# One head-group step of an attention kernel in another order: one call with the values, transposes and score products rearranged, waits left out

## The reference

```
q = rope(layernorm(x) @ Wq)            # 32 heads of 8 columns
k, v = split(ctx @ Wkv);  k = rope(k)
w = softmax(q @ k.T / sqrt(8))         # per batch and head, 256 x 256
x = x + tanh(g_xattn) * ((w @ v) @ Wout + bout)
x = x + tanh(g_ffn) * experts(layernorm(x))   # 2 shared, 32 routed, 6 of them per token
```

## Time and profile before

| what | value |
|---|---|
| median of 3 runs | 475.64 us |
| profiled execution, its own time | 475.44 us |
| its span | 473.6 us |
| TensorE busy, of the span | 448.4 us (95%) |
| VectorE busy | 286.7 us (61%) |
| ScalarE busy | 199.0 us (42%) |
| first score product starts | 40.35 us |
| last normalisation ends | 187.45 us |

### The profile page before, as it was taken

The page is one execution under the profiler, slowest core; times in us unless marked ns, Lnnn a source line. Parts: engine busy times, 40 slices in busy tenths (PEclk is TensorE's granted clock), DMA queues, the critical chain, the costliest instruction groups (busy, mean ns, idle before and its releaser), DMA issues.

```text
span 473.6 us, 8151 instructions
## 1 busy us (share of the span) xinstructions
PE 448.4 (95%) x2515; PEld 335.4 (71%) x2515; DVE 286.7 (61%) x574; ACT 199.0 (42%) x366; POOL 144.1 (30%) x233
## 2 busy tenths in 40 slices
PE   5788999999999998888899999999999999999996
PEld 5356666666666665566688888888888888888885
DVE  7897977877777674640445555455554455554455
ACT  1467777787877565471222222222222222222221
POOL 9046800000000000245144333444333444334430
PEclk9799999999999999999899999999999999999999
DMA  8012111111111100999852323333223322334102
GB/s 220 15 47 48 35 32 34 35 32 32 30 32 35 24 1 11 329 333 316 205 150 89 89 89 100 116 93 89 89 89 111 110 89 89 89 93 125 48 0 90
DMA packets 34056, 43.62 MB, mean 92 GB/s; under 512 B 5633, under 2 KB 28209, under 8 KB 34033
## 3 DMA queue, kind: packets, MB, share of 16 engines
q1 hardware_dynamic: 30737, 42.07, 31.1%
q10 hardware_dynamic: 3296, 1.25, 1.1%
HBM read 37.93 MB, written 1.18 MB: 83 GB/s over the span
## 4 chain that ended last, share of the span: by engine, by line
PE 85%; DVE 7%; ACT 3%; DMA 2%; issue 1%; POOL 1%; DVEq 0%; SPq 0%; POOLq 0%; ACTq 0%
PE psum L1126 26%; PE psum L1111 26%; PE psum L962 8%; PE psum L975 7%; PE psum L938 6%; PE psum L925 3%; PE psum L949 2%; PE psum L881 2%; PE psum L1024 2%; PE psum L890 1%; DVE nmax L716 1%; DVE ang L619 1%; PE psum L853 1%; PE psum L986 1%; DMA G<-gates_by_expert 1%
## 5 line engine op out<-in xcount | busy, mean ns | idle before, releaser
L591 ACT ACTIVATE hh<-hu 128x512 fp32r<-128x512 f32 x88 | 55.6, 633 | 186.7 <-DVE hu L822 186.7
L822 DVE SCALAR_TENSOR_TENSOR hu<-psum,b1cols,G 128x512 f32<-128x512 f32 x88 | 65.9, 751 | 110.3 <-PE psum L1111 101.3
L716 DVE TENSOR_REDUCE nmax<-psum 128x2 f32<-128x512 f32 x128 | 85.2, 687 | 25.9 <-PE psum L938 24.6
L492 ACT ACTIVATE probs<-psum 128x512 f32<-128x512 f32 x128 | 69.4, 595 | 14.1 <-PE psum L962 13.7
L1126 PE MATMUL psum<-hh,w2h 128*128 128x512 f32 (+1 forms) x188 | 73.3, 390 | 1.3 <-DVE hl L828 1.3
L1126 PE MATMUL psum<-hl,w2h 128*128 128x512 f32 (+1 forms) x188 | 73.2, 389 | 0.0
L1126 PE MATMUL psum<-hh,w2l 128*128 128x512 f32 (+1 forms) x188 | 73.1, 389 | 0.0
L828 DVE SCALAR_TENSOR_TENSOR hl<-hu,hh 128x512 fp32r<-128x512 f32 x88 | 60.3, 687 | 9.6 <-ACT hh L591 9.6
L1111 PE MATMUL psum<-xTh,w1h 128*128 128x512 f32 (+1 forms) x188 | 58.8, 394 | 2.2 <-POOL w1l L405 1.5
L1111 PE MATMUL psum<-xTh,w1l 128*128 128x512 f32 (+1 forms) x188 | 58.8, 394 | 0.0
L1111 PE MATMUL psum<-xTl,w1h 128*128 128x512 f32 (+1 forms) x188 | 58.5, 392 | 0.0
(11 more groups left out here) (148 smaller groups left out, 550.3 us busy)
## 6 DMA issues: line engine op xcount, KB each, us to landing
G<-gates_by_expert SPq DMA_DIRECT2D x40, 256.0 KB, 3.9
w<-in_L_ffn_rw_dram SPq DMA_DIRECT2D x4, 1408.0 KB, 13.4
w<-in_L_ffn_rw_dram SPq DMA_DIRECT2D x2, 2816.0 KB, 17.5
G<-gates_by_expert SPq DMA_DIRECT2D x8, 448.0 KB, 3.5
Kd<-QK SPq DMA_DIRECT2D x104, 32.0 KB, 1.9
G<-gates_by_expert SPq DMA_DIRECT2D x8, 384.0 KB, 3.5
G<-gates_by_expert SPq DMA_DIRECT2D x8, 320.0 KB, 3.4
G<-gates_by_expert SPq DMA_DIRECT2D x8, 192.0 KB, 3.7
```

The costliest lines, as they stand in the source:

```text
L492: act.activation(probs[g % 2][:, kt, 2 * hp:2 * hp + 2, :], ST_BANK[(4 * g + n) % 3][:, :].rearrange("p (h q) -> p h q", h=2), ACT.Exp, sc ...
L591: act.activation(hh[(SHT + j) % 2][:, cols], hu[2 * j + half][:, :], ACT.Relu).then_inc(rhh_ok, 1)
L716: dve.tensor_reduce(nmax[i % 2][:, qt, 2 * hp:2 * hp + 2], S_BANK[n % 2][:, :].rearrange("p (h k) -> p h k", h=2), AX.X, ALU.max, negate=T ...
L822: dve.scalar_tensor_tensor(out=hu[2 * (j % 2) + half][:, :], in0=H_BANK[2 * (j % 2) + half], scalar=b1cols[:, bass.ds(it * len(G) + j, 1)] ...
```

## The change

Six things change, all in the attention loop.

1. `values(i)` is one call: the eight matmuls of both halves follow one another, and each half still waits for its exponentials.
2. TensorE's order in a step is new. A step begins with `scores(i, 2)`. T2 stands between this product and `scores(i, 3)`. The first two products of the next group stand between shifted scores. The transposes for the group 3 ahead stand in front of the last shifted score.
3. ScalarE copies `oT` before a step's four exponentials, which follow one another.
4. VectorE takes all four row maxima and `maxima` before it normalises. `variances` of batches 0 to 2 moves behind the loop.
5. Transposed attention, projection and residual of batches 0 to 2 move to steps 11, 19, 27 and 12, 20, 28. The tile `attnT` lies in two other places of `Vx` for this.
6. Waits that others imply are left out. The wait for the copied keys moves from the first score product to the second transpose of T2, a step earlier than the keys are read, and at the start to the third product.

Before the change the first such residual stands behind step 28's maxima. The diff, cut to its core:

```diff
@@ constants
-        ATTN_STEPS = [GROUPS - 5, GROUPS - 3, GROUPS - 1]
-        PROJ_STEPS = [GROUPS - 4, GROUPS - 2, GROUPS - 1]
-        RESIDUAL_STEPS = [GROUPS - 4, GROUPS - 2, GROUPS - 1]
+        ATTN_STEPS = [NG * (b + 1) + 3 for b in range(B - 1)]
+        PROJ_STEPS = [n + 1 for n in ATTN_STEPS]
+        RESIDUAL_STEPS = PROJ_STEPS
@@ ScalarE, step(i)
                     evacuate_t(i + AHEAD)
-                if 0 <= g < GROUPS:
-                    exponentials(g, 0)
-                    exponentials(g, 1)
                 p = (i - 3) // 2
                 if i % 2 and 0 <= p < PAIRS:
-                    act.wait_ge(pv_mm, 2 * (i - 1))
-                    if p >= 2:
-                        act.wait_ge(ot_mm, p - 1)
+                    act.wait_ge(pv_mm, i - 1)
                     act.activation(oT[p % 2][:, :], O_BANK[:, 0:N], ACT.Copy).then_inc(o_ok, 1)
-                if i in ATTN_STEPS[1:]:
+                if i in ATTN_STEPS:
                     transposed_attention(ATTN_STEPS.index(i))
                 if 0 <= g < GROUPS:
-                    exponentials(g, 2)
-                    exponentials(g, 3)
-                if i == ATTN_STEPS[0]:
-                    transposed_attention(0)
+                    for n in range(4):
+                        exponentials(g, n)
@@ VectorE
                     row_max(i, 2)
+                    row_max(i, 3)
+                    maxima(i)
                 if i >= 4 and i % 2 == 0:
                     normalise((i - 4) // 2)
-                if i < GROUPS:
-                    row_max(i, 3)
-                    maxima(i)
                 if i in RESIDUAL_STEPS:
                     residual(RESIDUAL_STEPS.index(i))
-                if i == RESIDUAL_STEPS[-1]:
-                    variances(0, NT - TB)
+
+            variances(0, NT - TB)
@@ TensorE, transposed_with_max(i)
-                if i >= 1:
-                    pe.wait_ge(q2_ok, i)
...
                 for t in range(TB):
+                    if t and i + 2 < GROUPS:
+                        keys_copied(i + 2)
                     ins = pe.transpose(T2_BANK[:, t * P:(t + 1) * P],
@@ TensorE, values
-            def values(i, kt):
+            def values(i):
...
+                for kt in range(TB):
+                    pe.wait_ge(exp_ok, 4 * i + 2 * (kt + 1))
+                    for h in range(GH):
@@ TensorE, the loop
                 if i == 0:
+                    keys_copied(0)
                     scores(i, 0)
                     scores(i, 1)
-                if weighted:
-                    values(i - 2, 0)
+                    transposes(AHEAD)
+                    keys_copied(1)
+                if new:
+                    scores(i, 2)
                 if shifted:
                     transposed_with_max(i - 1)
...
                 if new:
-                    scores(i, 2)
+                    scores(i, 3)
+                if weighted:
+                    values(i - 2)
+                if i in ATTN_STEPS:
+                    attention_transposed(ATTN_STEPS.index(i))
+                if i in PROJ_STEPS:
+                    output_projection(PROJ_STEPS.index(i))
                 if i >= 4 and i % 2 == 0:
                     outputs((i - 4) // 2)
+                if i + 1 < GROUPS:
+                    scores(i + 1, 0)
                 if shifted:
                     shifted_scores(i - 1, 0)
                     shifted_scores(i - 1, 1)
...
+                if i + 1 < GROUPS:
+                    scores(i + 1, 1)
                 if shifted:
                     shifted_scores(i - 1, 2)
+                if i + 1 + AHEAD < GROUPS:
+                    transposes(i + 1 + AHEAD)
+                if shifted:
                     shifted_scores(i - 1, 3)
```

More of the change, by code:

```diff
@@ L964, in shifted_scores @@
                 ins.then_inc(st_mm, 1)
-            def values(i, kt):
+            def values(i):
                 b, g = i // NG, i % NG
-                pe.wait_ge(exp_ok, 4 * i + 2 * (kt + 1))
                 second = i % 2
-                if kt == 0 and not second and i:
-                    pe.wait_ge(o_ok, i // 2)
-                for h in range(GH):
-                    ins = pe.matmul(O_BANK[HR * h:HR * h + HR, 0:N], Vx[:, TB * b + kt, GH * g + h, :], probs[i % 2][:, kt, h, :],
-                                    start=(kt == 0 and not second), stop=(kt == TB - 1 and bool(second)),
-                                    skip_group_check=True)
+                for kt in range(TB):
+                    pe.wait_ge(exp_ok, 4 * i + 2 * (kt + 1))
+                    for h in range(GH):
+                        ins = pe.matmul(O_BANK[HR * h:HR * h + HR, 0:N], Vx[:, TB * b + kt, GH * g + h, :], probs[i % 2][:, kt, h, :],
+                                        start=(kt == 0 and not second), stop=(kt == TB - 1 and bool(second)),
+                                        skip_group_check=True)
                 ins.then_inc(pv_mm, 1)
             def outputs(p):
-                pe.wait_ge(o_ok, p + 1)
-                pe.wait_ge(q2_ok, min(2 * p + 4, GROUPS))
-                if p:
+                if 2 * p + 4 <= GROUPS:
+                    pe.wait_ge(q2_ok, 2 * p + 4)
+                else:
+                    pe.wait_ge(o_ok, p + 1)
                     pe.wait_ge(norm_ok, p)
```

49 lines of the change are left out of this document (13 added, 36 removed).

## The result

The changed kernel takes 468.98 us (median of 4, 467.25 to 470.71), before takes 475.35 (median of 4, 474.84 to 475.83): ratio 0.9866 [0.9827, 0.9906], 6.4 us less. Two later series of the changed kernel, 469.59 and 469.33, lie just inside it, so on which side of 469.0 the kernel falls is a matter of the runs' spread; the term that was off is not. The profiled execution took 467.25 us, its span is 465.2.

What follows compares the result with a forecast made beforehand. TensorE bounds the attention loop (busy 103.86 of 104.00 us) and stays the bound, narrowly. Terms -9.75 + 1.2 + 4.45 + 0.6 = -3.5 us take 475.44 to 471.9, or 472.1 against the median; range 469.0 to 476.8.

Steps and rivals of the forecast that it cites:

- The step: Attention loop: mean step 3.85 us against 4.176, saving 0.325 in each of 30 steps, -9.75 us.
- rival B: Inside merged `values`: a weight load of 0.11 stands open in each of 30 calls, 3.3 us back, 475.4; chance 0.12.
- Its parts: Within a step: one merged `values` call saves 0.27 us, and `QT` no longer in a hurry saves about 0.07.
- The margin of 0.1 for VectorE: Two row maxima end 0.35 into the next step, and `scores(i,3)` wants that bank at 0.45.
- Attention and projection: Steps 11 to 13 and their like, three batches: 6.95 us of stalls against 2.5 before, +4.45 us.
- the sign that the prediction had named for being wrong in the stalls: Step 12, with the projection: less than 1.9 us lost there would show the stalls wrong.
- rival C: Exponentials end the step: at 0.65 each, 0.2 to 0.25 us a step is lost, 478.6, slower; chance 0.13.
- the two waits for `QK`: TensorE waits for `QK`, copied near 2.1 us into a step: 0.35 lost in step 11, 0.4 in step 12.
- The start: Third product waits 0.5 us for group 1's keys; T2 of group 1 is 0.9 to 1.4 late: +1.2 us.
- The end: Group 31's exponentials queue behind group 30's; T2 to last normalisation goes from 6.8 to 7.4 us: +0.6.
- The waits left out: Attention loop: they cost nothing before, since each was met when its matmul came: 0.
- Rival E: Projection steps stall no more than before, since VectorE catches up: 4 us more gained, 468.1; chance 0.09.

Runs made afterwards that it cites:

- e1: Kernel before with only the merge of both `values` halves, all else in the old order: 474.29 us, ratio 0.9978.
- e2: Changed kernel with `values` in two halves again, the next group's first score product between them, except in attention and projection steps: 478.96 us, ratio 1.01.
- e8: Changed kernel with scores(i+1, 1) moved behind the last shifted score, so two score products stand side by side again: 483.89 us, ratio 1.0163.
- e4: Changed kernel with `outputs` ahead of the projection: 468.45 us, ratio 0.983.
- e6: Changed kernel with `outputs` ahead of the projection and the statistics of batches 0 to 2 in step 32: 465.97 us, ratio 0.9769.
- e7: Changed kernel with all the waits that the change left out put back: 470.29 us, ratio 0.9885.
- a0_again: The changed kernel timed again, nothing edited: 469.59 us, ratio 0.9873.
- e3_late_proj: Changed kernel with attention, projection and residual of batches 0 to 2 back near the loop's end (steps 27 to 32): 469.64 us, ratio 0.988.
- e5: Changed kernel with the statistics of batches 0 to 2 moved to step 32: 467.87 us, ratio 0.9835.
- e9: Changed kernel with `outputs` ahead of the projection, statistics in step 32 and the start's keys wait in front of scores(1, 0): 463.88 us, ratio 0.9751.
- a1_again: The changed kernel timed once more, nothing edited: 469.33 us, ratio 0.9884.

## Why the prediction was right in sign and too high

- **The step** (-9.75): right. 3.74 and 3.96 were forecast, 3.74 and 3.91 measured; -30 x 0.348 = -10.4, so 0.7 us more. The inner edge of `values` is free: its sets start 0.24, 0.22 and 0.22 us apart, with no load of 0.11 between the second and the third. That refutes rival B.
  The Trainium skill's "TensorE: Matmul & The Clock Gate" (Part 3, "What overlaps and what doesn't") has weight loads overlap only where row groups differ; here rows are the same, columns differ, and the sixteen loads took nothing of the 1.00 us, so the measurement decides.
- **Its parts** (merge 0.27, `QT` 0.07): they do not stand alone. The merge by itself gave 0.1 a step (e1), taking it out of the new order cost 0.39 to 0.47 (e2). The sum was right because the places of the score products, which I had priced at nothing, keep VectorE's banks in time; moving one back costs 0.63 (e8). The margin of 0.1 for VectorE held, barely: in the step shown above its second row maximum is over at 107.51 and the product that wants the bank starts at 107.63.
- **Attention and projection** (+4.45, from 6.95 us of stalls): the step that failed, by size. By the same sum as in the prediction, 30 x 3.828 - 1.8 + 6.5 = 119.5, and 124.98 were taken: 5.4 us of stalls, not 6.95; less the 2.5 of before, +2.9. Step 12 lost 1.42, not 1.9 (the sign that the prediction had named for being wrong in the stalls), step 11 nothing, not 0.35. Read step by step, steps 11 to 13 lost 1.5, 19 to 21 the same and 27 to 29 2.2, together 5.2. (The sum of the prediction leaves out that the changed kernel has one call of transposes and one product less in this stretch, 0.67 us; about as much is lost while the loop runs out, in steps 30 and 31.)

  The cause is the copy `QK`, which the prediction had TensorE wait for in both steps. I had it end 2.1 us into a step, and it ends at 1.64. Of these 0.46 us, 0.20 are that I gave the four exponentials the 2.26 us of a row in which TensorE fed them; the two copies behind them take 0.17 less than I had assumed (0.77 for 0.94), and the block starts 0.1 sooner. Back to back the exponentials take 2.06:

```profile
106.07 2.06 ACT L488 ACTIVATE probs<-psum 128x512 f32<-128x512 f32 x4 [1.08 <-PE psum L948]
108.00 0.42 ACT L496 ACTIVATE QT<-psum 128x256 fp32r<-128x256 f32 x1
108.26 0.64 ACT L447 ACTIVATE QK<-psum 128x512 fp32r<-128x512 f32 x1
```

  `QK` is there at 108.90, 1.64 us behind the third product's 107.26, before `values` ends, so neither step waits for it. It also leaves ScalarE 0.4 us of room (the block ends at 108.13, the second half of `values` starts near 108.52), which takes rival C away. The rest, VectorE's chain, was named rightly, and e4 to e6 show it. By starts, step 12 loses 0.55 us at the bank of `transposes` (0.5 forecast) and 0.72 + 0.11 at the product behind the row maxima (0.8), and step 13 0.13 (0.2). So the two waits for `QK`, 0.35 + 0.4 in each of three batches or 2.25 us, are the terms that were not there.
- **The start** (+1.2): +0.26 in the profile of the result. The third product stood 1.38 us behind the first and 1.28 before, so the keys cost 0.10 there, not 0.5; in the three slow starts it was 0.45 to 0.67. And I added the wait to a path that I took to be free of others. Before has its own stall there: T2 of group 0 at 44.16 and of group 1 at 48.14, 3.98 apart against 3.31 after. The term is not one number: 0.26 mostly, 2.3 to 2.5 in three profiles of ten, for the reasons given under the start.
- **The end** (+0.6): +0.51, by the mechanism named. Exponentials of group 31 queue behind group 30's, and the halves of `values` come apart again:

```profile
171.62 0.64 PE L960 MATMUL psum<-probs,Vx 128*32 128x256 f32 x8
172.44 0.16 PEld L960 LDWEIGHTS psum<-probs,Vx 128*32 128x32 f32 x8 [0.66 <-ACT probs L488]
```

  `variances` is hidden, with 0.65 us to spare (half a us forecast):

```profile
180.52 2.03 DVE L646 TENSOR_SCALAR Vx<-x_sb,mv,rstd 128x256 f32<-128x256 f32 x6
183.20 0.75 DVE L739 SCALAR_TENSOR_TENSOR x_sb<-psum,gx,x_sb 128x512 f32<-128x512 f32 x1 [0.65 <-PE psum L1013]
```

- **The waits left out** (0): right (e7).

So 0.7 for the step, 1.55 for the stalls, 0.95 for the start and 0.1 for the end make 3.3 us, and 0.43 behind the loop go the other way: 2.9 of the 3.1 us by which the forecast was too high. Rival E had nearly the time (468.1) by luck, with the wrong cause, since the projection steps do stall more than before, by 2.9 us, and even that could be had (e6). Four terms erred to one side, and two of them, the stalls and the start, by more than the bounds that I had given them (1 us, and 0.9 to 1.4).

## What to carry to other kernels

When a step's engines all have a little time left, an order is worth what it does to the moments at which each engine gets its input: the merge alone gave nothing that can be told from the runs (0.2%), merge and new order together 1.3%, and with one product out of place the kernel lost 1.6% on before. Take a duration for a queue of like instructions from a row in which nothing fed them late. A step with extra work on one engine needs its short dependents ahead of the long matmuls and what nobody waits for moved out of it.

## What the runs showed of the hardware

**VectorE beside GpSimd's memsets.** A small VectorE operation in SBUF that meets GpSimd's memsets can last until one of them ends. The first of the program, before (VectorE, then GpSimd):

```profile
4.21 5.45 DVE L619 TENSOR_SCALAR ang<-pos_sb 128x16 f32<-128x16 f32 x1 [1.21 <-DMA pos_sb<-in_fside_BxSx_dram]
7.04 2.60 POOL L329 MEMSET Vx<- 128x2944 f32 x1
```

It ends at 9.66, the memset at 9.64. In the changed kernel's profile the same operation took 0.97 us, from 4.20 to 5.17, and in `a0_again` 8.17. In all 18 profiles it ends 0.03 us behind the end of a memset, and near one of three times: 5.16, 9.66 or 12.41. In the five profiles with the first of these the first score product starts at 37.49 to 38.63, in the other thirteen at 39.92 to 41.38. So this is where the -2.07 us of the table's first line come from: the statistics behind these operations start at 13.39 in before and at 10.47 in the changed kernel's profile, and the transposes behind the statistics at 20.75 and 18.66, 2.09 apart. The Trainium skill's "SBUF — State Buffer" ("SBUF: two separate sides") calls it an exclusive lock on a shared pair of ports, held for a whole instruction. The trace agrees for the end, and shows besides that VectorE can lose it to several memsets in a row.

**TensorE's clock can fall behind short waits.** It was 1.00 through the loop of before. In `a0_again` TensorE waited 1.31 us for row maxima up to 164.35, in step 28, and what followed ran lower (windows, columns as in the first fence):

```profile
162.00:166.00 4.00, 2.69 (x22) 1.54 (x24) 3.93 (x8) 2.34 (x5) 0.00 (x0) 0.97 0.03 8
166.00:170.00 4.00, 4.00 (x26) 2.92 (x18) 2.03 (x6) 2.05 (x5) 0.00 (x0) 0.61 0.00 0
```

That is 1.2 GHz for most of the second stretch, and the step after took 4.99 us, where the changed kernel's first profile has 3.70. That profile has the same wait of 1.31 us in step 28, up to 160.34, and its clock stayed at 1.00 behind it: what decides is not shown. Of the twelve profiles with such a projection step three had it behind step 28 (`a0_again`, `e3_late_proj`, `e8_products_together`), of the four in which its chain was cut (e4, e5, e6, e9) none. A wait of 1.3 us can cost as much again. Of the six runs of `a1_again` the three above 470 us had a mean clock of 0.981 to 0.984, the three below it of 0.988 to 0.993, which would fit. But the runs of before spread as wide (472.71 to 477.90 us beside `a0_again`, those up to 473.3 with clocks of 0.991 or more, those above 477 with 0.983 to 0.986), with a clock of 1.00 through the loop of its profile, so how much of the changed kernel's spread of 6 us comes from this is not shown.
